# Key sums over quarters of the queries, and 37 attention turns an image in place of 25

## The reference, cut to what matters

```
x = x + window_attention_and_mlp(group_norm(x))     # 7 x 7 windows, 4 heads
t = x as 3136 tokens of an image                    # 16 images
n = layer_norm(t)
q, k, v = n @ Wq + bq, n @ Wk + bk, n @ Wv + bv     # 32 channels, one head
t = t + n + softmax(q @ k.T / sqrt(32)) @ v         # 3136 x 3136 scores an image
t = t + mixture_of_experts(layer_norm(t))
```

## Time and profile before

| | |
|---|---|
| median of 3 runs | 2871.67 us (2868.67 to 2872.39) |
| span of the profiled execution | 2864.1 us |
| total time of the profiled execution | not given apart from its span |
| TensorE busy | 2715.3 us, 95% |
| VectorE busy | 2279.2 us, 80% |
| ScalarE busy | 2075.1 us, 72% |
| window stage, prep | up to about 760 us, then to about 830 us |
| attention | from about 855 to about 2760 us |
| one image of it | 118.7 us |

### The profile page before, as it was taken

The page is one execution under the profiler, slowest core; times in us unless marked ns, Lnnn a source line. Parts: engine busy times, 40 slices in busy tenths (PEclk is TensorE's granted clock), DMA queues, the critical chain, the costliest instruction groups (busy, mean ns, idle before and its releaser), DMA issues.

```text
span 2864.1 us, 60666 instructions
## 1 busy us (share of the span) xinstructions
PE 2715.3 (95%) x25297; PEld 1265.9 (44%) x25297; DVE 2279.2 (80%) x2943; ACT 2075.1 (72%) x3927; POOL 621.5 (22%) x506
## 2 busy tenths in 40 slices
PE   4899999999689999999999999999999999999987
PEld 3455555555333434434344343443444434444337
DVE  4899999999388788787887877878788787887844
ACT  4688889888547777777777777777777777777762
POOL 0566666666001010110100101101011010110100
PEclk6899999999879999999999999999999999999997
DMA  3000000000480101011010110101101001010003
GB/s 99 7 24 19 25 19 24 19 24 24 174 251 1 24 1 24 1 24 24 1 24 2 22 24 1 24 9 16 24 1 24 15 10 24 1 24 1 1 1 92
DMA packets 92580, 82.21 MB, mean 29 GB/s; under 512 B 61108, under 2 KB 82197, under 8 KB 91285
## 3 DMA queue, kind: packets, MB, share of 16 engines
q1 hardware_dynamic: 92085, 78.29, 10.4%
q10 hardware_dynamic: 224, 0.07, 0.0%
HBM read 39.60 MB, written 32.11 MB: 25 GB/s over the span
## 4 chain that ended last, share of the span: by engine, by line
PE 84%; ACT 7%; DVE 5%; issue 2%; DMA 1%; SPq 1%; POOL 0%; POOLq 0%; ACTq 0%; DVEq 0%
PE ps L1685 21%; PE ps L1658 19%; PE ps L1708 19%; PE ps L1718 3%; PE ps L1487 3%; DVE arena L1150 3%; PE ps L1506 2%; PE ps L1670 2%; PE ps L1479 2%; PE ps L1497 2%; PE ps L1518 2%; ACT arena L882 1%; PE ps L1763 1%; ACT arena L734 1%; PE ps L1534 1%
## 5 line engine op out<-in xcount | busy, mean ns | idle before, releaser
L1261 DVE TENSOR_REDUCE arena<-ps 128x2 f32<-128x896 f32 (+1 forms) x1408 | 1454.7, 1078 | 354.1 <-PE ps L1658 354.0
L902 ACT ACTIVATE arena<-ps 128x512 f32<-128x512 f32 (+1 forms) x2464 | 1268.9, 602 | 347.2 <-PE ps L1685 333.8
L1685 PE MATMUL ps<-arena 97*128 97x512 f16 x2800 | 818.5, 356 | 10.8 <-ACT arena L902 1.2
L1658 PE MATMUL ps<-arena 96*128 96x448 f16 x2800 | 771.6, 357 | 11.1 <-DVE arena L1251 8.6
L1708 PE MATMUL ps<-arena 128*32 128x512 f32 (+2 forms) x7328 | 666.6, 456 | 0.7 <-DVE arena L1283 0.7
L1685 PEld LDWEIGHTS ps<-arena 97*128 97x128 f16 x2800 | 251.1, 99 | 441.1 <-ACT arena L902 183.6
L1708 PEld LDWEIGHTS ps<-arena 128*32 128x32 f32 x7328 | 238.0, 109 | 406.7 <-ACT arena L902 200.7
L631 POOL TENSOR_TENSOR tok<-arena,tok 128x128 f32<-128x128 f32 (+1 forms) x112 | 47.6, 425 | 1540.1 <-DVE arena L1283 1540.1
L1658 PEld LDWEIGHTS ps<-arena 96*128 96x128 f16 x2800 | 226.7, 99 | 286.3 <-DVE arena L1261 101.5
L576 POOL TENSOR_TENSOR arena<-arena 113x784 f32<-113x784 f32 x128 | 192.6, 1505 | 156.5 <-DVE arena L1126 156.5
L571 POOL TENSOR_TENSOR arena<-arena 113x784 f32<-113x784 f32 x128 | 192.6, 1505 | 86.0 <-DVE arena L1115 85.9
(11 more groups left out here) (184 smaller groups left out, 2520.7 us busy)
## 6 DMA issues: line engine op xcount, KB each, us to landing
arena<-qk_scratch SPq DMA_DIRECT2D x96, 196.0 KB, 4.0
qk_scratch<-arena SPq DMA_DIRECT2D x16, 448.0 KB, 5.2
arena<-ximg SPq DMA_DIRECT2D x16, 400.0 KB, 7.0
arena<-in_x SPq DMA_DIRECT2D x4, 1568.0 KB, 10.8
xa_scratch<-arena SPq DMA_DIRECT2D x32, 196.0 KB, 1.9
res_scratch<-arena SPq DMA_DIRECT2D x32, 196.0 KB, 2.0
arena<-xa_scratch SPq DMA_DIRECT2D x4, 1568.0 KB, 8.3
arena<-res_scratch SPq DMA_DIRECT2D x4, 1568.0 KB, 12.0
```

Of the source, the lines that this page charges most:

```text
L902: act.activation(pk[0:rows, x % DEPTH, QC * m:QC * m + n], ps[0:rows, w % SB, 0:n], ACT.Exp, scale=float(C) ** -0.5).then_inc(att["exp"], 1)
L1261: dve.tensor_reduce(mxp[0:rows, p, 2 * u:2 * u + k], ps[0:rows, at_:at_ + k, 0:KN], AX_X, ALU.max)\
L1658: last = pe.matmul(ps[:, MB + 2 * (j % 2) + n % 2, 0:KN], q2[p][0:96, T * t:T * t + T], k2[p][0:96, KN * m:KN * m + KN], start=True, stop= ...
L1685: last = pe.matmul(ps[:, bank, at_ % QC:at_ % QC + chunk_cols(c)], k2[p][0:97, T * t:T * t + T], q2[p][0:97, QC * c:QC * c + chunk_cols(c) ...
```

## The change

Each full chunk's key sums now hold a quarter of the queries in each column tile: every key tile is four products of 128 columns. The four column tiles then need no adding up, the sums are 128 x 128, `sums_copy` copies 128 columns in place of 512, and `out_values` is one product with `wv4`, a block-diagonal weight of four `wvo`, in place of four. For that the queries must be in the order (i q) from the start: `by_rows` reads them with a stride of four in the projection, which now goes by chunks of 512 columns. A full chunk has six turns of 2, 2, 2, 2, 2 and 3 steps (4, 4, 4, 4, 4 and 5 scores), so an image has 37 turns. The pairs of maxima are spread over them by their number of scores: two or three a turn. With these numbers, turns 0, 3, 8, 13, 18, 22, 27 and 32 of an image have four scores and three pairs, the turns of five scores have three pairs, all others two. Output products stand in turns 0, 1, 7, 13, 19, 25 and 31. The rows of maxima stand in turns 4, 10, 16, 22, 28, 30 and 36 (before: 3, 7, 11, 15, 19, 20 and 24 of 25).

```diff
-        ua = carve(QC)
+        ua = carve(T)
+        wv4 = wsmall[:, :, :, :].rearrange("p k j c -> p (k j c)")[:, 0:4 * (C + 1)]
+        def by_rows(v, n):
+            return v.rearrange("p (q i) -> p i q", i=4) if n == QC else v
...
-            starts = [*range(0, n - 1, 3)]
+            starts = [*range(0, n - 1, 2)]
...
-        OUT_PLACE = {6: 3, 7: 3, 4: 2}
+        OUT_PLACE = {4: 2, 5: 2}
-        PLACES = {(6, 3): (1, 3, 5), (6, 4): (0, 2, 4, 6), (7, 3): (1, 3, 5), (7, 4): (1, 3, 5, 7)}
+        PLACES = {(4, 2): (1, 3), (4, 3): (0, 2, 4), (5, 2): (1, 3), (5, 3): (1, 3, 5)}
...
# stores of prep, high_part, low_part, project_group: pieces of 512 columns (the last 64) for 448
+                w = slice(QC * a_, min(QC * z, S))
-                        sp.dma_start(qk_g[k, g, :, KN * a_:KN * z], hl[:, k, KN * a_:KN * z]).then_inc(prep[done], 16)
+                        sp.dma_start(qk_g[k, g, :, w], hl[:, k, w]).then_inc(prep[done], 16)
...
+                x = xgr[g % 2][:, QC * n:QC * n + w]
+                pe.matmul(ps[:, j % 8, 0:w], wqk[:, i, :], by_rows(x, w) if i == 0 else x, start=True, stop=True)\
...
# sums_copy
-                if n == QC:
-                    act.activation(ua[:, :].rearrange("p (i q) -> p i q", i=4),
-                                   ps[:, AVB, :].rearrange("p (q i) -> p i q", i=4), ACT.Copy).then_inc(att["acopy"], 1)
-                else:
-                    act.activation(ua[:, 0:n], ps[:, AVB, 0:n], ACT.Copy).then_inc(att["acopy"], 1)
+                w = min(n, T)
+                act.activation(ua[:, 0:w], ps[:, AVB, 0:w], ACT.Copy).then_inc(att["acopy"], 1)
...
# setup, VectorE
+            dve.tensor_tensor(wv4.rearrange("p (j c) -> p j c", j=4), bcast(wvo[:, :], 4),
+                              cv("blk4").rearrange("p (j o) -> p j o", o=1).broadcast_to([128, 4, C + 1]), ALU.mult)
...
# key_sums
-                full = c < NQ - 1
-                turn_of = [k for k in turns if x in k][0]
-                alone = full and (len(turn_of) == 3 and x == turn_of[2])
-                for i, (t, at_) in enumerate(tiles):
-                    parts = 4 if t == NT - 1 and full else 2 if alone else 1
-                    w = n // parts
-                    for h in range(parts):
-                        g = h if parts == 4 else 2 * i + h if parts == 2 else (2 * (turn_of.index(x) % 2) + i if full else t % 4)
-                        last = pe.matmul(ps[C * g:C * (g + 1), AVB, w * h:w * h + w], vf[p][:, t, :],
-                                         pk[:, x % DEPTH, at_ + w * h:at_ + w * h + w],
-                                         start=(t < 4), stop=(t >= NT - 4), skip_group_check=True)
+                for t, at_ in tiles:
+                    if n == QC:
+                        for g in range(4):
+                            last = pe.matmul(ps[C * g:C * (g + 1), AVB, 0:T], vf[p][:, t, :],
+                                             pk[:, x % DEPTH, at_ + T * g:at_ + T * (g + 1)],
+                                             start=(t == 0), stop=(t == NT - 1), skip_group_check=True)
+                    else:
+                        g = t % 4
+                        last = pe.matmul(ps[C * g:C * (g + 1), AVB, 0:n], vf[p][:, t, :], pk[:, x % DEPTH, at_:at_ + n],
+                                         start=(t < 4), stop=(t >= NT - 4), skip_group_check=True)
...
# out_values
-                for q in chunk_tiles(c):
-                    i = q % 4
-                    last = pe.matmul(ps[:, AVB, (C + 1) * i:(C + 1) * (i + 1)], ua[:, T * i:T * i + T], wvo[:, :],
-                                     start=True, stop=True)
+                n = min(chunk_cols(c), T)
+                w = C + 1 if n < T else 4 * (C + 1)
+                pe.matmul(ps[0:n, AVB, 0:w], ua[:, 0:n], wvo[:, :] if n < T else wv4, start=True, stop=True)\
+                  .then_inc(att["out"], 1)
```

More of the change, by code:

```diff
@@ L860, in high_part @@
                     act.wait_ge(prep["stored_a" if n < 4 else "stored_b"], 64 * g)
-                act.activation(hl[:, 2 * i, KN * n:KN * n + KN], ps[:, j % 8, 0:KN], ACT.Identity, bias=bqk[:, i:i + 1])\
+                w = chunk_cols(n)
+                act.activation(hl[:, 2 * i, QC * n:QC * n + w], ps[:, j % 8, 0:w], ACT.Identity, bias=bqk[:, i:i + 1])\
                    .then_inc(prep["hi"], 1)
@@ L1227, in low_part @@
                     dve.wait_ge(prep["stored_a" if n < 4 else "stored_b"], 64 * g)
-                dve.scalar_tensor_tensor(hl[:, 2 * i + 1, KN * n:KN * n + KN], ps[:, j % 8, 0:KN], bqk[:, i:i + 1],
-                                         hl[:, 2 * i, KN * n:KN * n + KN], ALU.add, ALU.subtract).then_inc(prep["lo"], 1)
+                w = chunk_cols(n)
+                dve.scalar_tensor_tensor(hl[:, 2 * i + 1, QC * n:QC * n + w], ps[:, j % 8, 0:w], bqk[:, i:i + 1],
+                                         hl[:, 2 * i, QC * n:QC * n + w], ALU.add, ALU.subtract).then_inc(prep["lo"], 1)
             def residual_copy(g, n):
@@ L1715, in out_values @@
                 pe.wait_ge(att["acopy"], b * NQ + c + 1)
-                for q in chunk_tiles(c):
-                    i = q % 4
-                    last = pe.matmul(ps[:, AVB, (C + 1) * i:(C + 1) * (i + 1)], ua[:, T * i:T * i + T], wvo[:, :],
-                                     start=True, stop=True)
-                last.then_inc(att["out"], 1)
+                n = min(chunk_cols(c), T)
+                w = C + 1 if n < T else 4 * (C + 1)
+                pe.matmul(ps[0:n, AVB, 0:w], ua[:, 0:n], wvo[:, :] if n < T else wv4, start=True, stop=True)\
+                  .then_inc(att["out"], 1)
             def image_steps(b, p, first=False, last=False):
@@ L1762, in project_group @@
                 free_bank(j)
-                pe.matmul(ps[:, j % 8, 0:KN], wqk[:, i, :], xgr[g % 2][:, KN * n:KN * n + KN], start=True, stop=True)\
+                w = chunk_cols(n)
+                x = xgr[g % 2][:, QC * n:QC * n + w]
+                pe.matmul(ps[:, j % 8, 0:w], wqk[:, i, :], by_rows(x, w) if i == 0 else x, start=True, stop=True)\
                   .then_inc(prep["proj"], 1)
```

## The result

The changed kernel takes 2847.89 us (2846.25 to 2848.89, 4 runs) against 2871.28 (2868.67 to 2872.39) on the same chip: a ratio of 0.9922, 95% interval 0.9908 to 0.9936. It is faster by 23 us, 0.8%: clear of the noise, but small. The forecast said 58 faster, 2814. The direction and the range held, the size did not.

The account below looks back on a forecast made before the run. The order on TensorE was taken to set the time; the attention terms summed to -3.7 us an image, -59 for 16 images, and with the small terms outside gave 2871.7 - 58 = 2814 us, range 2784 to 2856.

Parts of the forecast that it names:

- rival C: Rival, 17%: waits for banks and rings do not shrink, so the bank-wait gain is nothing; +2.6 us x 16, 2856.
- Outside the attention: Projection: queries read with a stride of four on TensorE, taken as +1 us, up to 21 if speed halved.
- 1: Key sums on TensorE: passes take columns x 2 / 2.4 + 2.5 ns; 34.8 to 32.7 us, gain 2.1 an image.
- 2: Switches into and out of key-sum blocks: 37 in place of 25, 12 x (0.10 + 0.14) = +2.9 us an image.
- 3: Output product on TensorE: 0.25 us in place of 0.81, six times, gain 3.4 us an image.
- 4: TensorE's waits for a score bank: 3.9 us an image before, 1.3 after, gain 2.6.
- 7: VectorE's bursts, two 0.98 us sums over an image's tokens in short turns: +0.3 us an image, between 0 and 1.2.
- 5: Row of maxima before a new chunk: five rows each lose 0.15 us by coming one turn earlier, gain 0.8 an image.
- 6: A chunk's first key sums wait for the bank that `weighted` frees: five waits of 0.40 us, +2.0 an image.
- A: Rival, 7%: a weight load is exposed ahead of each 128-column pass; +7.5 us an image, 2934.
- B: Rival, 14%: the new wait for the bank `weighted` frees is not there; -2.0 us x 16, 2782.
- D: Rival, 5%: upper ends of the `weighted` wait and VectorE's bursts cancel the gain; 2908 us at worst.

Follow-up runs that it names:

- e1: Changed kernel with TensorE reading the queries' projection contiguously, ScalarE and VectorE making the order when reading PSUM; 2828.42 us, ratio to before 0.985.
- e2: Kernel before, with only the queries' projection reading its moving operand with a stride of four; 2888.14 us, ratio 1.0057.
- e4: Changed kernel with the turns of the kernel before (three or four steps, 25 an image), keeping the new key sums and single output product; 2803.18 us, ratio to before 0.9759.
- e5: Changed kernel, 37 turns, with the contiguous queries' projection and `weighted` ahead of the maxima; 2797.6 us, ratio to before 0.9742.
- e6: Changed kernel with 25 turns an image and the contiguous queries' projection; 2788.47 us, ratio to before 0.9708.
- e3: Changed kernel with VectorE's `weighted` put ahead of the maxima at place 1 of the same turn; 2814.37 us, ratio to before 0.9801.

## Why the prediction was wrong

Two things failed, about equally: the price of the strided read outside the attention (1 us in the sum, some 19 measured), and several terms inside it that were each a little too good. An image came out at 116.2, not 115.0. Added up, 16 x 1.2 + 18 = 37 us too little gain; 34 were missing (the first image gained 4.3 us and the last 3.1, the others 2.5). Of the 1.2 an image, 0.5 is the row of maxima, 0.5 the waits for banks and ring, 0.2 the new wait and 0.1 the output products, within 0.1. That the direction was right owes nothing to luck, but that the time still fell inside the range does: its upper end was drawn for rival C, whose mechanism did not occur. By its own steps:

**Outside the attention: the single term that failed most.** "The queries are read with a stride of four; a strided f32 moving operand ... took 555 ns against 545 ... I take +1." The line of the earlier trace rows reads a window, seven elements in a row and then a step; it never takes every fourth element. It was the wrong nearest row, and its 64 rows for 128 made it no better match. The upper bound written beside it, 21 us, was what happened on TensorE (24 x 0.93 = 22), and it was carried neither into the sum nor into a rival. e1 and e2 settle the size, 19 and 15 us in the runs and 19 to 21 in the traces.

**1 and 2, key sums and switches: right.** The law for passes held: 1.02 for four tiles, 1.23 for five, 1.67 for seven in e4. Entering still costs 0.09 and leaving 0.14.

**3, output product: right.** 0.23 for 0.25. The small chunk's product became dearer, 0.23 and 0.09 of entering for 0.14; 0.2 an image that no step had. It now has 64 columns of weights where it had 128; that this is the cause, no run shows.

**4 and 7, waits for banks and ring: somewhat too good.** By subtracting 0.217 a score, 0.19 a product of 448 columns and 0.09 an entry from every row of an image, waits inside the turns were 3.6 us before and are 1.8 after, beside those for `weighted`. The forecast had 3.9 and 1.6, and so a gain of 2.3 for 1.8. The turn in which VectorE sums over an image's tokens shows the worst, 0.78 for a score pair in place of 0.43 (TensorE, the changed kernel), with VectorE's maxima named as releaser:

```profile
1964.53 0.60 PE L1693 MATMUL ps<-arena 97*128 97x512 f16 x2
1965.31 0.55 PE L1666 MATMUL ps<-arena 96*128 96x448 f16 x2 [0.19 <-DVE arena L1269]
```

**5, row of maxima: less than half, and for another reason.** It now costs its block 0.22 in six turns and 0.03 in the seventh, whose row is one product of 64 columns: 1.4 an image. Before, it cost 0.37 in four turns, 0.19 in one and nothing in two, where it stood in the unbalanced end of a turn of four, with two column tiles that had nothing to do: 1.7. So it gained 0.3, not 0.8. Nor was it the earlier turn that gained: in e4 the rows stand in the old turns, and cost 0.22 as well. TensorE, e4, a block of three steps with its row of maxima, 1.68 from start to start where 1.45 is usual (1.80 and 1.43):

```profile
1916.93 0.65 PE L1710 MATMUL ps<-arena 128*32 128x128 f32 x16
1917.41 0.22 PE L1678 MATMUL ps<-negid,mq 128*1 128x128 f16 x1
...
1917.64 1.04 PE L1710 MATMUL ps<-arena 128*32 128x128 f32 x26
1918.61 0.39 PE L1693 MATMUL ps<-arena 97*128 97x512 f16 x1
```

The 0.15 a row belongs to the old form of the sums; what in it cost them stays open.

**6, the new wait: right in mechanism and place,** 0.49 in four turns and 0.26 in the small chunk's, 2.2 in all, for five times 0.40. What was short was the way from the end of `weighted` to the start of the block, 0.14 in place of 0.05 to 0.09; it is 0.14 or 0.15 in all 79 such waits of the trace.

**What the forecast did not ask.** It priced each step against the kernel before and never summed the steps that belong to the turns alone: +2.9 of switches, +2.2 of waiting, against 2.1 saved in bank waits (3.9 in e4, 1.8 with 37 turns), which is 3.0 for the 2.8 by which the image of e4 is shorter. Had it done so with its own numbers (+2.9 + 2.0 + 0.3 - 2.6 - 0.8 = +1.8), it would have said that 37 turns cost 29 us, and that the gain lies in the form of the sums and the output product. e4 measured 45. With VectorE's order mended the split still costs 0.7 us an image (e5 against e6), 9 us in the runs.

**The rivals.** A, an exposed weight load: refuted, 32 passes in 1.02. B, no wait at step 6: refuted by the row that names line 1291, and by e3, which removes it. C, bank waits that stay: not so, they halved (3.6 to 1.8); its time, 2856, is closer to the measured one than the forecast, but for another reason. D, upper ends of 6 and 7: refuted, 0.49 a turn for 1.4.

**The rule.** A block of 32 passes, eight deep in each column tile, takes 1.02 us, the law's time to 0.01. By the Trainium skill's rule ("TensorE: Matmul & The Clock Gate", Part 3, The mechanism: a weight load overlaps a running product only where the row group differs) eight weight loads of an estimated 27 ns (32 columns / 1.2, the page's section LDWEIGHTS) would add 0.2 to it. The trace disagrees with the rule here too. The same section also lets a load go ahead into a background weight buffer, which the prediction left out; the trace does not speak against that.

Left open: why the first profile of the kernel before was 9.5 us shorter than the second. 5.2 us of it lie ahead of the second image, 0.2 in the images, and 4.1 behind them; no run was made for that.

## What to carry to other kernels

Where a change regroups work and alters its form too, sum each separately before believing in either; here the form was worth some 85 us in the attention (83 in the runs, e6 against before), the strided read took about 19 of them back and the regrouping 45, of which 34 were VectorE's order (e3). When an in-order engine gets shorter turns, look at what its neighbours hold in their own order: a result that another engine waits for belongs ahead of bulk work that has slack. And do not price an access pattern by a row whose pattern is only called strided; take the row with the same step, or carry the bound into the range.

## What the runs showed of the hardware

- An f32 moving operand (128 rows) read with a step of 16 bytes streams at half speed: 1.79 for 0.86 us at 512 columns, 1.56 for 0.76 at 448. With a step of 8 bytes it is 0.80 for 0.75 at 448.
- The same step of 16 bytes costs ScalarE nothing in reading PSUM (0.69 us for 512 columns, either way), nor VectorE (0.74 to 0.75, either way).
- Passes of 128 columns in four column tiles hold 109 ns each for at least 14 in a row (56 passes in 1.67 us with 0.14 of entering and leaving the form), with a weight load for every one.
- TensorE starts 0.14 us after the end of the VectorE instruction that it waited for (`weighted`, 79 times in the changed kernel).
